# Extra bf16 products on TensorE in the waits of local attention and gated feed-forward

## The reference

```python
for i in range(DEPTH):            # DEPTH = 6
    x = attn_layer(shift_tokens(x), Wqkv[i], q_scale[i], k_scale[i], Wo[i]) + x
    x = ffn_layer(shift_tokens(x), ln_g[i], ln_b[i], W1[i], b1[i], W2[i], b2[i]) + x
```

## Time and profile before

| | us |
|---|---|
| median of three runs | 4640.06 |
| lowest, highest | 4635.36, 4648.96 |
| the profiled execution | 4643.98 |
| its span, first to last instruction | 4641.7 |

### The profile page before, as it was taken

The page is one execution under the profiler, slowest core; times in us unless marked ns, Lnnn a source line. Parts: engine busy times, 40 slices in busy tenths (PEclk is TensorE's granted clock), DMA queues, the critical chain, the costliest instruction groups (busy, mean ns, idle before and its releaser), DMA issues. The chain is left out here.

```text
span 4641.7 us, 153206 instructions
## 1 busy us (share of the span) xinstructions
PE 4208.2 (91%) x50948; PEld 2773.1 (60%) x50950; DVE 3754.6 (81%) x9044; ACT 3499.6 (75%) x12855; POOL 3200.6 (69%) x4297
## 2 busy tenths in 40 slices
PE   6949899998999989999899998999989999777885
PEld 3426566664666646666466664666646666555543
DVE  4779899984999749997599965999669995688497
ACT  6938788883888838887488874888658886588434
POOL 2522299992999839997499964999659995344172
PEclk9969999999999989999999999999989999788886
DMA  2000000000000000000000000000000000000000
GB/s 61 0 21 0 6 2 0 0 1 25 2 0 0 1 25 2 0 0 20 6 2 0 0 20 6 2 0 0 20 6 1 0 0 20 1 0 0 28 1 19
DMA packets 36132, 34.43 MB, mean 7 GB/s; under 512 B 11302, under 2 KB 31012, under 8 KB 34852
## 3 DMA queue, kind: packets, MB, share of 16 engines
q1 hardware_dynamic: 35876, 31.13, 2.2%
HBM read 29.03 MB, written 2.10 MB: 7 GB/s over the span
## 5 line engine op out<-in xcount | busy, mean ns | idle before, releaser
L2226 ACT ACTIVATE local_prob<-ps,local_shift_by 128x128 f32<-128x128 f32 x3072 | 1078.5, 377 | 10.4 <-DVE local_shift_by L2318 10.3
L2154 POOL TENSOR_TENSOR local_qk<-local_qk,local_rsin 128x512 f32<-128x512 f32 x768 | 968.0, 1271 | 56.5 <-DVE local_rsin L2343 56.4
L2161 POOL TENSOR_TENSOR local_qk<-local_qk,local_inv 128x512 f32<-128x512 f32 x768 | 792.4, 1043 | 135.3 <-ACT local_inv L2245 134.5
L2477 PE MATMUL ps<-local_wqkv,local_xsT 128*128 128x512 f32 x1536 | 828.2, 625 | 51.1 <-DVE local_rsin L2343 24.9
L2168 POOL TENSOR_TENSOR local_prob<-local_prob,local_rs 128x512 f32<-128x512 f32 x768 | 789.8, 1040 | 12.3 <-DVE local_rs L2325 12.3
L2226 ACT ACTIVATION_READ_ACCUMULATOR local_prob<-ps,local_shift_by 128x1 f32 x3072 | 671.3, 219 | 0.0
L2318 DVE TENSOR_REDUCE local_shift_by<-ps 128x4 f32<-128x512 f32 x768 | 524.8, 683 | 86.0 <-PE ps L2553 86.0
L2343 DVE TENSOR_TENSOR local_rsin<-ps,local_sin_t 128x256 f32<-128x256 f32 x1536 | 572.2, 414 | 0.0
L2332 DVE TENSOR_TENSOR local_qk<-ps,local_cos_t 128x512 f32<-128x512 f32 x768 | 525.4, 684 | 48.8 <-ACT local_sq L2234 46.4
L2234 ACT ACTIVATE local_sq<-ps 128x512 f32<-128x512 f32 x768 | 466.8, 608 | 99.5 <-PE ps L2477 79.1
L2350 DVE TENSOR_REDUCE local_ss<-local_sq 128x8 f32<-128x512 f32 x768 | 513.5, 670 | 5.9 <-ACT local_sq L2234 5.9
(11 more groups left out here) (336 smaller groups left out, 8663.1 us busy)
## 6 DMA issues: line engine op xcount, KB each, us to landing
local_wqkv<-L_ffn_Wqkv SPq DMA_DIRECT2D x7, 1536.0 KB, 6.5
local_wo<-L_ffn_Wo SPq DMA_DIRECT2D x7, 512.0 KB, 7.1
out<-quantised_res SPq DMA_DIRECT2D x8, 256.0 KB, 2.3
local_w<-L_ffn_W SPq DMA_DIRECT2D x6, 341.0 KB
early_L_decay<-c_decay SPq DMA_DIRECT2D x1, 1024.0 KB, 11.0
local_w<-L_ffn_W SPq DMA_DIRECT2D x12, 64.0 KB
load_raw<-L_ffn_w SPq DMA_DIRECT2D x8, 64.0 KB, 2.0
local_b<-L_ffn_b SPq DMA_DIRECT2D x24, 0.5 KB
```

What stands on the lines that cost most here:

```text
L2154: nc.gpsimd.tensor_tensor(qk[w][:, j, :, :], qk[w][:, j, :, :], rsin[j % 2][:, :, :], ALU.add).then_inc(rot_ready, 1)
L2161: nc.gpsimd.tensor_tensor(qk[w][:, j, :, :], qk[w][:, j, :, :], bcast(inv[:, w, 8 * j:8 * j + 8].unsqueeze(2), [P, 8, LH]), ALU.mult).then ...
L2226: last = nc.scalar.activation(prob[w][:, g, j, :], ps[:, 4 + g % 2, j * P:(j + 1) * P], ACT.Exp, bias=shift_by[:, w, h:h + 1], accum_out=s ...
L2477: nc.tensor.matmul(proj_bank(j), xsT[w][:, :], wqkv[:, 512 * j:512 * j + 512], start=True, stop=True).then_inc(proj_ready, 1)
```

## The change

A helper `keep_busy` issues a number of bf16 products of the identity and the band matrix, 512 columns each, into a PSUM bank whose content is not read before it is written anew. Nothing waits for them and they raise no semaphore; they stand in TensorE's own list. In `gated_ffn` three stand at the start, five behind the first transposes and five behind the loop, all into bank 2. In `local_attention` they go to bank 6: three behind the first transpose, ten, eleven and nine ahead of projections (0, 2), (1, 0) and (1, 2), eleven ahead of the first scores of batch 0, and eight behind the loop. What is computed stays the same.

```diff
--- before.py
+++ after.py
@@ -126,6 +126,13 @@
 def heads8(ap):
 
     return ap.rearrange("p (h d) -> p h d", d=DH)
+
+
+def keep_busy(nc, env, bank, times):
+
+    for _ in range(times):
+        nc.tensor.matmul(bank.rearrange("p (h q) -> p h q", q=P), env["identb"][:, :],
+                         bcast(env["band"][:, :].unsqueeze(1), [P, bank.shape[1] // P, P]), start=True, stop=True)
 
 
 def block_diagonal(tile):
@@ -1996,6 +2003,8 @@
 
         @block.tensor
         def _(pe):
+            SPARE = ps[:, 2, :]
+            keep_busy(nc, env, SPARE, 3)
             if kind == "L1":
                 pe.wait_ge(env["ffn_loaded"], mine)
 
@@ -2029,8 +2038,11 @@
                     for t in range(QUAD):
                         last = nc.tensor.transpose(T[:, t * P:(t + 1) * P], xin[1 - u][:, t, :], ident[:, :])
                     last.then_inc(turned, 1)
+                    if isinstance(b, int) and b == 0:
+                        keep_busy(nc, env, SPARE, 5)
                 hidden(2)
             sequence_loop(pe, NQ, 2, 1, step)
+            keep_busy(nc, env, SPARE, 5)
     ph.close(env)
 
 
@@ -2442,6 +2454,8 @@
                 nc.tensor.matmul(ps[:, 4 + p, :].rearrange("p (h k) -> p h k", h=HG), identb[:, :],
                                  bcast(band[:, :].unsqueeze(1), [P, HG, P]), start=True, stop=True)
 
+            SPARE = ps[:, 6, :]
+
             def turn_x(b, w, live):
                 if live(b):
                     pe.wait_ge(xin_ready, b + 1)
@@ -2450,9 +2464,15 @@
                         wait(pe, shift_ready, b - 5)
                         wait(pe, xsT_ready, b)
                     nc.tensor.transpose(OUT[:, P:2 * P], xin[w][:, :], ident[:, :]).then_inc(turned, 1)
+                    if isinstance(b, int) and b == 0:
+                        keep_busy(nc, env, SPARE, 3)
+
+            FILL = {(0, 2): 10, (1, 0): 11, (1, 2): 9}
 
             def project(b, w, j, live):
                 if live(b):
+                    if isinstance(b, int) and (b, j) in FILL:
+                        keep_busy(nc, env, SPARE, FILL[(b, j)])
                     if j == 0:
                         pe.wait_ge(xsT_ready, b + 1)
                         wait(pe, rot_step, 4 * b)
@@ -2527,6 +2547,8 @@
 
             def scores(b, w, half, live):
                 if live(b):
+                    if isinstance(b, int) and b == half == 0:
+                        keep_busy(nc, env, SPARE, 11)
                     if half == 0:
                         waits_alone(pe, env, (qkT_ready[half][0], b + 1), (qkT_ready[half][1], b + 1),
                                     (exp_ready, 4 * b - 1), (exp_ready, 4 * b))
@@ -2649,6 +2671,7 @@
                 project(n, u, 2, live)
                 scores(n - 2, u, 1, live)
             sequence_loop(pe, NB, 0, 5, step)
+            keep_busy(nc, env, SPARE, 8)
     ph.close(env)
```

## The result

The changed kernel takes 4614.65 us (median of 4, 4613.38 to 4615.17), the kernel before in the same comparison 4638.59 us (4635.36 to 4648.96). The ratio is 0.9939 with a 95% interval of 0.9927 to 0.9951: 28 us or 0.6% faster, between 23 and 34 us. The profiled execution took 4615.17 us, 28.8 us less than that of before.

The account below looks back on a forecast made before the run. TensorE was taken to bound the local layers (busy 403.5 of 405.0 us), its clock falling after waits. Terms -18 - 16.8 - 0.9 + 2.5 = -33.2 us took the 4640.06 us median to 4607 us, range 4590 to 4628.

Parts of the forecast that it names:

- The fill: Start of the six local attention layers: added products fit inside TensorE's waits and keep the clock up, 18 us saved.
- the 11 products ahead of the first scores: Local layers: cost taken as 0.2 us, bounds nothing to 2.4 us, because VectorE's maximum stands behind its own queue.
- further falls of the clock: Local layers: one in two or three may keep one more fall, 1 to 1.5 us; 20.2 us became 18.
- The first layer: First local layer: 1 us more than the other layers' 491.3 us, since its lead-in is another stage.
- rival 2: All added products: the clock stays low under them, 0.43 us each, kernel at 4730 us; chance 0.04.
- the prediction's own signs of being wrong: Projection right behind an added product without wait, 0.50 stretches holding added products, or (2,1) starting later than 25.4 us.
- Into the gated stage: Six seams from local layers: first hidden product 0.51 us sooner, then full clock saves 2.24 us; 16.8 us saved.
- The stage of the third pair: Gated stage of L2, entered with the clock already low: 0.9 us saved, ends -2.5 and +2 us.
- Out of the gated stage: Seven seams behind gated stages: five added products end 0.35 us behind VectorE's residual, 2.5 us lost.
- Rival 4: Fill and gated seams: all low-clock time is given back at half, 63 us, kernel at 4580 us; chance 0.06.
- rival 3: Whole kernel: the clock falls about as often, only later, and gains cancel losses; 4638 us, chance 0.09.
- Rival 1: Local fill: TensorE's queue counts, so products before the first scores cost 13 us in six layers; 4620 us, chance 0.12.

## Why the prediction was right, and where it was off

*The fill.* Its steps hold in the trace of the changed kernel nearly to the tenth of a microsecond: (0,2), (1,0) and (1,2) were put at 5.98, 11.08 and 15.62 us from the layer's start and stand at 5.96, 11.07 and 15.50; the scores at 20.6, measured 20.74; (2,1) at 24.05, measured 24.2. The term was 18 us, measured 17.5 against the same profile of before.

*The term that was mis-sized* is that of the 11 products ahead of the first scores: "I take 0.2, nearest the low end, because VectorE's next need of those scores, the maximum at 2292.07, stands behind its own queue". VectorE in the changed kernel, fourth layer, and in the one without these products:

```profile
2277.57 0.69 DVE L2330 TENSOR_REDUCE local_shift_by<-ps 128x4 f32<-128x512 f32 x1
...
2279.28 0.69 DVE L2378 COPY local_vals<-ps 128x512 f32<-128x512 f32 x1 [0.36 <-PE ps L2513]
```

```profile
2270.82 0.68 DVE L2330 TENSOR_REDUCE local_shift_by<-ps 128x4 f32<-128x512 f32 x1
...
2272.02 0.68 DVE L2378 COPY local_vals<-ps 128x512 f32<-128x512 f32 x1
```

The maximum did stand behind VectorE's queue: it starts 21.78 us into the layer with the products and 21.62 without. But behind the scores TensorE also has the transposes and the value projection (line 2513), and VectorE must copy the values out before (2,1). For that copy it waits for TensorE with the products, and not without: it starts at 23.49 instead of 22.82, and the layers are 0.5 to 0.7 us longer. In six layers the term is 3 to 4 us and not 1.2. Priced right alone, it had put the forecast at about 4609.

It hardly shows in the term's sum, and that is luck. The forecast had 20.2 us by its steps and kept back 2.2 for further falls of the clock. None came; instead layers two to six stand 0.3 us above the 491.3 of the steps and the first 1.25 us above its 492.3, 2.7 us in all. The wait ahead of the scores in which the clock still fell was called (1,1) there; it is (1,0).

*The first layer* was put 1 us above the others, at about 492.3; it took 493.55. TensorE in order of time at its start, where the clock comes in low from the cross attention (start 563.84):

```profile
564.89 1.48 PE L134 MATMUL ps<-band,identb 128*128 128x512 bf16 x3
566.17 3.54 PE L2497 MATMUL ps<-local_wqkv,local_xsT 128*128 128x512 f32 x4
```

Three products take 1.48 us there instead of 0.81 and stand in front of the projections, which begin 0.37 us later than before. It is rival 2 in one place, and one of the prediction's own signs of being wrong: a low stretch that holds added products. In this profile the clock came back at 5.7 us, no sooner than in the second profile of before. In the kernel without the gated tail, whose first layer is the same, it came back at 2.8 us and the layer took 491.61, so 493.55 is not the layer's fixed time.

*Into the gated stage.* The forecast had the 3 products hidden, xT 0.53 us sooner, and the 5 done just before the first hidden product, with that product at 2.27 us from the start. All engines at the fourth one (start 2747.39), against the earlier trace rows:

```profile
2745.12 1.89 PE L134 MATMUL ps<-band,identb 128*128 128x512 bf16 x8
...
2746.75 0.35 DVE L2409 TENSOR_SCALAR XN<-local_xs,local_moments,local_rstd 128x128 f32<-128x128 f32 x1 [0.37 <-ACT local_rstd L2269]
...
2747.42 0.81 PE L134 MATMUL ps<-band,identb 128*128 128x512 bf16 x3 [0.41 <-PEq L2132]
...
2748.15 0.63 PE L2039 MATMUL ps<-ident,L_gated_xin 128*128 128x128 f32 x4
...
2748.61 1.24 PE L134 MATMUL ps<-band,identb 128*128 128x512 bf16 x5
...
2748.87 0.78 ACT L1959 ACTIVATE L_gated_xT<-ps,local_ln_b,local_ln_g 128x512 f32<-128x512 f32 x1 [2.16 <-PE ps L2039]
...
2749.70 1.13 PE L2019 MATMUL ps<-L_gated_xT,local_w 128*128 128x512 f32 x2
```

The product stands at 2749.70, 2.31 us, and the stage is 2.68 us shorter where 2.75 were reckoned; six stages gave 16.7 for 16.8. The stage of the third pair gave 0.7 for 0.9.

*Out of the gated stage*, against the earlier trace rows:

```profile
2817.32 1.24 PE L134 MATMUL ps<-band,identb 128*128 128x512 bf16 x5
2817.52 0.69 DVE L2000 TENSOR_TENSOR Y<-L_gated_xb,ps 128x512 f32<-128x512 f32 x1 [3.04 <-PE ps L2031]
...
2818.86 0.59 PE L2454 MATMUL ps<-band,identb 128*128 128x512 bf16 x2 [0.30 <-PEq L1920]
```

From VectorE's residual's start to the next stage's first product it is 1.34 us where it was 1.01: 0.33 us for 0.35, seven times 2.3 for 2.5.

*The whole.* The touched stages and seams give 32.6 us in the two profiled executions that the sum was made for, against 33.2. The ratio says 28 us with an interval of 23 to 34, which holds both. Two things in the profiles point to less than 32.6: 3.3 us of other clock in the first attention stage, present in the second profile of before as well, and a first profile of before whose touched stages were longer than in the second (2969.0 and 2966.3, 441.6 and 440.8). Whether they make up the difference isn't shown.

The rule of the Trainium skill, "TensorE: Matmul & The Clock Gate", section "Terms", that throttled time costs its length times one minus the clock's ratio, would make 3.4 us of a gated stage's 6.8 us at 0.50. The stage became 2.7 us shorter, with the 0.5 us of the earlier start in it, so the rule is somewhat high there and far too high in the fill: there the low time of the six layers, 109 us, fell to 26, and 17.5 us came of it, 0.21 us for each and not 0.5. Rival 4 fell with that, rival 3 with the clock's row of the first 33.9 us. Rival 1 was right in that the products reach the layer's end, and wrong in the amount. Of rival 2, 11 of the 403 added products ran low: three at the first layer's start and the eight at the start of the third pair's gated stage.

## What to carry to other kernels

Work that nobody reads can hold TensorE's clock, and it pays where it lies wholly inside a wait and TensorE is the bound behind it: the groups here leave 0.4 to 0.6 us of each wait, and what was put beyond that ahead of projection (1,0) came back in full as time of the layer. Price each group by the whole chain behind the product it delays, not by its first reader, and give a group that stands where there is no wait little credit for what it may prevent: without the eleven ahead of the first scores the clock fell in their place in 2 of 12 layers, and they cost 0.5 to 0.7 us in each. Where a stage is entered with the clock already low, products in front of its work run low too and cost about twice (1.48 us for three in place of 0.81). Trim behind the last product of a stage by what the seam already waits for: three were free, five cost 0.33 us, none let the clock stay low longer in one layer of six. Compare stages that run the same instructions first: a layer that the edit didn't touch differed by 1.9 us between two profiles, more than most of the terms looked for.

## What the runs showed of the hardware

The clock's falls differ from one execution to the next in the same kernel: a layer of the unchanged kernel took 495.40 us in one profile and 493.19 in another. With the waits filled the layers two to six lay within 0.6 us of each other, and the four runs of the changed kernel within 1.8 us (4613.38 to 4615.17) where those of before spread over 13.6 us. The later variants spread over 2 to 7 us in four to ten runs each, the kernel before over 10 to 16 us in seven to seventeen, so the change takes away scatter as well as time. Products of 64 columns at the same number held the clock at one seam (into the local layers from the second on) and not at the other (into the gated stage). Broad ones ran 0.215 us apart at 1.00 (22 in 4.91 us), and three of them took 1.48 us together at 0.50. A low stretch near 34 us cost a layer 0.9 to 1.1 us for its 3.4 us (491.59 against 490.72 with the first scores' products, 491.05 against 489.99 without).
